# One core, a retention layer with an fp4 feed-forward: the attention output kept with its columns on partitions

## What is computed

```python
q, k = rope(x @ Wq), rope(x @ Wk)                  # 8 heads of 16
v, g = x @ Wv, x @ Wg                              # 8 heads of 32, together 256 columns
decay = where(diff >= 0, exp2(diff * s_head), 0)   # causal, one rate per head
o = (q k^T * 16**-0.5 * decay) v                   # no softmax
o = o * rsqrt(mean(o * o, over the head's 32) + 1e-5) * g_norm_w
attention = (o * silu(g)) @ Wo
ffn = fp4(silu(fp4(x1) Wgate^T) * (fp4(x1) Wup^T)) Wdown^T   # weights fp4 too, blocks of 16, width 352
```

## Time and profile before

| | us |
|---|---|
| median of 3 runs | 139.93 (139.84 to 140.35) |
| the profiled execution | 139.86 |
| its span, first to last instruction | 137.9 |
| TensorE busy | 122.2 (89%) |
| VectorE busy | 112.5 (82%) |
| ScalarE busy | 98.2 (71%) |
| GpSimd busy | 96.6 (70%) |

### The profile page before, as it was taken

The page is one execution under the profiler, slowest core; times in us unless marked ns, Lnnn a source line. Parts: engine busy times, 40 slices in busy tenths (PEclk is TensorE's granted clock), DMA queues, the critical chain, the costliest instruction groups (busy, mean ns, idle before and its releaser), DMA issues.

```text
span 137.9 us, 3502 instructions
## 1 busy us (share of the span) xinstructions
PE 122.2 (89%) x1224; PEld 78.1 (57%) x1224; DVE 112.5 (82%) x391; ACT 98.2 (71%) x311; POOL 96.6 (70%) x139
## 2 busy tenths in 40 slices
PE   4964998999999999999999999999999958888660
PEld 4822454657556465666667675757575735445550
DVE  1269468959778899999999999999999899999710
ACT  3055266678778796887888879797888978876763
POOL 4213727877876958888787979797979797656561
PEclk9999559999999999999999999999999999999997
DMA  3899980000000000000000000000000000000022
GB/s 116 255 250 233 412 257 8 0 5 5 0 5 0 0 5 2 0 5 2 0 0 5 0 2 24 0 19 7 19 0 19 5 19 19 19 21 19 19 59 60
DMA packets 6897, 6.53 MB, mean 47 GB/s; under 512 B 864, under 2 KB 6112, under 8 KB 6752
## 3 DMA queue, kind: packets, MB, share of 16 engines
q1 hardware_dynamic: 5856, 5.56, 13.6%
q10 hardware_dynamic: 1024, 0.76, 1.7%
HBM read 5.26 MB, written 1.05 MB: 46 GB/s over the span
## 4 chain that ended last, share of the span: by engine, by line
PE 78%; DVE 9%; ACT 7%; issue 2%; POOL 2%; POOLq 1%; ACTq 0%; DVEq 0%
PE ps L338 13%; PE ps L355 8%; PE ps L483 6%; PE ps L467 6%; PE ps L395 6%; PE ps L329 5%; PE ps L460 5%; PE ps L385 4%; PE ps L474 3%; PE ps L368 3%; PE ps L411 3%; PE ps L403 2%; PE ps L420 2%; PE ps L419 2%; ACT hT L513 2%
## 5 line engine op out<-in xcount | busy, mean ns | idle before, releaser
L900 POOL TENSOR_TENSOR rstd_h<-ms,minus_half 128x8 f32<-128x8 f32 x16 | 26.4, 1649 | 8.4 <-DVE ms L765 7.7
L891 POOL TENSOR_TENSOR qk<-rope_c,rope_s 128x256 f32<-128x256 f32 x16 | 11.6, 728 | 14.4 <-DVE rope_s L742 14.3
L338 PE MATMUL ps<-w_vg,xT_sb 128*128 128x512 f32 x32 | 19.0, 676 | 0.0
L483 PE MATMUL ps<-wd_T,hT 128*128 128x128 f32 x96 | 13.6, 278 | 2.7 <-ACT hT L513 2.7
L738 DVE TENSOR_TENSOR rope_c<-ps,tabs_sb 128x256 f32<-128x256 f32 x16 | 6.8, 424 | 11.1 <-PE ps L329 11.1
L925 POOL TENSOR_TENSOR hq<-h_grid,hs 128x352 f32<-128x352 f32 x16 | 13.0, 814 | 3.0 <-DVE h_grid L678 3.0
L514 ACT ACTIVATE q_eo<-ps,consts 128x128 f32<-128x128 f32 x32 | 11.8, 370 | 3.5 <-PE ps L347 3.5
L355 PE MATMUL ps<-q_eo,kT 32*128 32x256 f32 x128 | 12.0, 444 | 2.5 <-ACT q_eo L514 2.5
L483 PEld LDWEIGHTS ps<-wd_T,hT 128*128 128x128 f32 x96 | 12.1, 193 | 3.5 <-DVE r L792 2.6
L513 ACT ACTIVATE raw<-ps 128x512 f32<-128x512 f32 x16 | 9.6, 599 | 6.1 <-PE ps L355 6.1
L895 POOL TENSOR_SCALAR_AFFINE_SELECT probs<-raw 128x512 f32<-128x512 f32 x16 | 10.2, 637 | 5.0 <-ACT raw L513 5.0
(11 more groups left out here) (112 smaller groups left out, 363.5 us busy)
## 6 DMA issues: line engine op xcount, KB each, us to landing
tabs_sb<-rope_tables SPq DMA_DIRECT2D x1, 1024.0 KB, 11.4
out<-x SPq DMA_DIRECT2D x16, 64.0 KB, 1.5
tabs_sb<-rope_tables SPq DMA_DIRECT2D x1, 640.0 KB, 8.0
xT_sb<-x_transposed SPq DMA_DIRECT2D x1, 512.0 KB, 9.4
x_res<-x SPq DMA_DIRECT2D x1, 512.0 KB, 12.0
xT_sb<-x_transposed SPq DMA_DIRECT2D x1, 320.0 KB, 6.6
x_res<-x SPq DMA_DIRECT2D x1, 320.0 KB, 8.6
w_vg<-in_w_vg ACTq DMA_DIRECT2D x1, 256.0 KB, 3.4
```

The costliest lines, as they stand in the source:

```text
L338: mm(vg_ps, xT(c), w_vg[:], start=True, stop=True).then_inc(vg_pe, 1)
L483: last = mm(down_ps, hT[:, c % 2, t, :], wd_T[:, t, :], start=t == 0, stop=t == 2)
L891: gp.tensor_tensor(qk[:, c % D, :], rope_c[:, c % D, :], rope_s[:, c % D, :], ALU.add).then_inc(qk_p, 1)
L900: gp.tensor_tensor(rstd_h[:, c, :], ms[:, c, :], minus_half[:], ALU.pow).then_inc(rms_p, 1)
```

## The change

The attention output stays with its columns on partitions. The transposes of o and y and the copies around them go. ScalarE squares oT straight from PSUM; TensorE sums each head's squares with a product against a 0/1 matrix of four columns (`mean_squares`; the sums have the rows of the chunk on partitions); VectorE adds the epsilon, GpSimd takes the power as before, ScalarE spreads each head's factor over its 32 columns (`spread_rstd`), TensorE transposes that (`transpose_rstd`), and VectorE multiplies it with the gated output (`gated_output`), which is yT directly. g is therefore computed transposed too, by two products with g's weights as the stationary side. MB is 1: VectorE masks two heads, ScalarE and GpSimd handle six. Four warm-up products follow the transposes of qk for chunks 0, 1 and 2. The lists of steps of all four engines are in a new order, with new offsets, and LAST is 31.

```diff
...
 HB = I // BLK
-MB = 2
+MB = 1
 EPS = 1e-5
...
     g = np.exp(C * lg[head])
-    cst = np.stack([head % 2 == 0, head % 2 == 1, 1 / g, g], 1)
+    cst = np.stack([head % 2 == 0, head % 2 == 1, 1 / g, g, *(row // DV == n for n in range(4))], 1)
     return tab.astype(f), cst.astype(f)
...
         oT_ps = ps[:, 0:2, 0:C]
-        o_ps = ps[:, 2, 0:VD]
-        yT_ps = ps[:, 3, 0:VD]
+        ms_ps = ps[:, 2, 0:NH]
+        rstd_ps = ps[:, 3, 0:2 * C].rearrange("p (g q) -> p g q", q=C)
         qk_ps = ps[:, 4, 0:256]
         qkT_ps = ps[:, 4, 256:512]
-        vg_ps = ps[:, 5, :]
+        v_ps = ps[:, 5, 0:VD]
+        gT_ps = ps[:, 5, VD:].rearrange("p (g q) -> p g q", q=C)
         att_ps = ps[:, 5, 0:H]
...
-        FIRST, LAST = -2, 28
+        FIRST, LAST = -2, 31
...
                 elif tile.get(bank) == "oT":
-                    pe.wait_ge(oT_act, filled["oT"])
-                elif tile.get(bank) == "o":
-                    pe.wait_ge(gate_v, filled["o"])
-                elif tile.get(bank) == "yT":
-                    pe.wait_ge(yT_act, filled["yT"])
+                    pe.wait_ge(sq_act, filled["oT"])
+                    pe.wait_ge(gate_v, filled["oT"])
+                elif tile.get(bank) == "ms":
+                    pe.wait_ge(ms_v, filled["ms"])
+                elif tile.get(bank) == "rstd":
+                    pe.wait_ge(yT_v, filled["rstd"])
...
                 for _ in range(n):
-                    mm(ps[:, 7, 0:C], ident[:], ident[:], start=True, stop=True)
+                    mm(ps[:, 6, 0:C], ident[:], ident[:], start=True, stop=True)
...
                 free_vg_bank()
-                mm(vg_ps, xT(c), w_vg[:], start=True, stop=True).then_inc(vg_pe, 1)
+                mm(v_ps, xT(c), w_vg[:, 0:VD], start=True, stop=True)
+                for g in range(2):
+                    last = mm(gT_ps[:, g, :], w_vg[:, VD + g * H:VD + (g + 1) * H], xT(c), start=True, stop=True)
+                last.then_inc(vg_pe, 1)
                 fill(5, "vg")
...
                 fill(4, "qkT")
+                if c < 3:
+                    warm_up(4)
...
-            def transpose_o(c):
+            def mean_squares(c):
...
                     free_scores_bank(2)
-                pe.wait_ge(oT_act, c + 1)
-                transpose(o_ps[:, 0:C], oT[:, c % 2, 0, :], ident[:])
-                transpose(o_ps[:, C:2 * C], oT[:, c % 2, 1, :], ident[:]).then_inc(tr_pe, 1)
-                fill(2, "o")
-            def transpose_y(c):
+                pe.wait_ge(d_cst, 16)
+                pe.wait_ge(sq_act, c + 1)
+                for g in range(2):
+                    last = mm(ms_ps[:, 4 * g:4 * g + 4], o_sq[:, c % 2, g, :], head_of_row, start=True, stop=True)
+                last.then_inc(ms_pe, 1)
+                fill(2, "ms")
+            def transpose_rstd(c):
...
                     free_scores_bank(3)
-                pe.wait_ge(y_p, c + 1)
-                transpose(yT_ps[:, 0:C], y[:, c % 2, 0:128], ident[:])
-                transpose(yT_ps[:, C:2 * C], y[:, c % 2, 128:256], ident[:]).then_inc(yT_pe, 1)
-                fill(3, "yT")
+                pe.wait_ge(spread_act, c + 1)
+                for g in range(2):
+                    last = transpose(rstd_ps[:, g, :], rstd_all[:, c % 2, 4 * g:4 * g + 4, :].rearrange("p h d -> p (h d)"),
+                                     ident[:])
+                last.then_inc(rstd_pe, 1)
+                fill(3, "rstd")
...
                 free_vg_bank()
-                pe.wait_ge(yT_act, c + 1)
+                pe.wait_ge(yT_v, c + 1)
                 mm(att_ps, yT[:, c % 2, 0, :], wo_s[:, 0, :], start=True, stop=False)
...
                 run = stage_runner(s)
+                run(up, -5)
+                run(transpose_h, -8)
+                run(transpose_rstd, -1)
+                run(from_state, 0)
                 run(state_product, 0)
                 run(values, 0)
-                run(transpose_y, -1)
                 run(transpose_xq, -4)
-                run(down, -8)
-                run(transpose_o, 0)
                 run(transpose_qk, 1)
                 run(out_projection, -1)
+                run(mean_squares, 0)
+                run(down, -8)
                 run(gate, -4)
...
                     transpose_down_weights()
-                run(up, -4)
                 if s == 2:
...
                 run(scores, 1)
+                run(project_qk, 2)
                 run(project_vg, 1)
-                run(transpose_h, -7)
-                run(project_qk, 2)
-                run(from_state, 1)
...
                 act.wait_ge(vg_pe, c + 1)
-                copy(v_sb[:, c % D, :], vg_ps[:, 0:VD])
-                nc.scalar.activation(silu_g[:, c % D, :], vg_ps[:, VD:2 * VD], ACT.Silu).then_inc(vg_act, 1)
+                copy(v_sb[:, c % D, :], v_ps)
+                nc.scalar.activation(silu_g[:, c % D, :, :], gT_ps, ACT.Silu).then_inc(vg_act, 1)
...
                 run = stage_runner(s)
-                if s == 1:
+                run(k_transposed, -2)
+                run(q_odd, -2)
+                run(q_even, -2)
+                run(magic_x, -6)
+                run(ln1_norm, -5)
+                if s == 5:
+                    copy_gate_up_weights()
+                run(ln2_norm, -14)
+                run(ln2_squares, -12)
+                run(silu_of_gate, -7)
+                run(copy_scores, -2)
+                run(spread_rstd, -3)
+                run(copy_v_and_silu, -2)
+                if s == 4:
                     weights_magic(1)
-                run(copy_oT, 0)
-                run(copy_yT, -1)
-                run(copy_xqT, -4)
-                run(squares, 0)
-                run(q_even, 1)
-                run(k_transposed, 1)
-                run(q_odd, 1)
-                run(magic_x, -3)
-                run(ln2_norm, -11)
-                if s == 2:
-                    copy_gate_up_weights()
+                run(copy_hT, -10)
                 if s == 3:
+                    weights_magic(0)
+                if s == 6:
                     copy_down_weights()
-                run(ln1_centre, -2)
-                run(silu_of_gate, -4)
-                run(ln2_squares, -9)
-                run(copy_scores, 1)
-                run(copy_v_and_silu, 1)
-                run(ln1_norm, -2)
-                run(copy_hT, -7)
-                if s == 0:
-                    weights_magic(0)
-                run(magic_h, -5)
+                run(magic_h, -8)
+                run(ln1_centre, -4)
+                run(squares, -2)
+                run(copy_xqT, -6)
...
-            def mean_square(c):
-                dve.wait_ge(sq_act, c + 1)
-                vec.tensor_reduce(ms[:, c, :], o_sq[:, c % 2, :, :], AX.X, ALU.add).then_inc(ms_v, 1)
+            def mean_square_eps(c):
+                dve.wait_ge(ms_pe, c + 1)
+                vec.tensor_scalar(ms[:, c, :], ms_ps, EPS, None, ALU.add).then_inc(ms_v, 1)
...
                 dve.wait_ge(sq_act, c + 1)
-                vec.tensor_tensor(gate_o[:, c % 2, :], o_ps, silu_g[:, c % D, :], ALU.mult).then_inc(gate_v, 1)
+                vec.tensor_tensor(gate_o[:, c % 2, :, :], oT_ps, silu_g[:, c % D, :, :], ALU.mult).then_inc(gate_v, 1)
+            def gated_output(c):
+                dve.wait_ge(gate_v, c + 1)
+                dve.wait_ge(rstd_pe, c + 1)
+                vec.tensor_tensor(yT[:, c % 2, :, :], gate_o[:, c % 2, :, :], rstd_ps, ALU.mult).then_inc(yT_v, 1)
...
                 run = stage_runner(s)
-                run(mean_square, -1)
-                run(gated, -1)
-                if s == 0:
+                if s == 1:
+                    weights_amax(0)
+                run(ln1_stats, -3)
+                if s == 1:
                     weights_inv(0)
-                run(x_plus_, -4)
-                run(ln1_sum, -2)
                 if s == 3:
+                    weights_grid(0)
+                run(ln2_sum, -10)
+                if s == 4:
+                    weights_plus(1)
+                run(x_plus_, -5)
+                if s == 2:
+                    weights_inv(1)
+                if s == 4:
                     weights_grid(1)
                 if s == 2:
-                    weights_plus(1)
+                    weights_ratio(1)
+                run(h_grid_, -8)
+                run(x_grid_, -5)
+                run(h_ratio_, -7)
+                run(mask_scores, -1)
+                run(ln1_aggr, -3)
+                run(x_amax, -4)
+                run(rotate, 0)
+                if s == 1:
+                    weights_amax(1)
+                run(h_product, -6)
+                run(x_inv, -4)
                 if s == 2:
-                    weights_grid(0)
+                    scale_wo()
                 if s == 1:
                     weights_ratio(0)
-                if s == 1:
-                    scale_wo()
-                run(h_grid_, -7)
-                run(x_grid_, -4)
-                run(h_ratio_, -6)
```

(97 more changed lines are left out.)

6 lines of the change are left out of this document (2 added, 4 removed).

## The result

The changed kernel takes 139.09 us in the median of 20 runs (139.04 to 139.65). The kernel before, run beside it 20 times, has 139.04 us (137.27 to 140.35). The ratio, by the executions that each kernel shows near its fastest, is 1.0065 (95% interval 1.0036 to 1.0094): slower by about 0.65%. The prediction said 138.1 us, 1.3% faster than 139.93. The time lies in the range of 136.0 to 141.2, the direction is wrong.

A forecast was written before the change was run, and what follows sets the result against it. TensorE bounds the steady part at 6.74 us per period, VectorE the end. 8.11 + 5.4 + 5.9 + 17.1 + 17.9 + 48.8 + 33.0 gives a span of 136.2, plus 1.96 makes 138.1 us; range 136.0 to 141.2.

The forecast's parts named there:

- the clock term: From scores(1) to scores(2): warm-ups keep TensorE's clock at full speed, so 5.9 us instead of 8.15, -2.2.
- 1.0 of early waits: In the stretches before the full steady periods: shorter waits on TensorE save 1.0 us in all.
- TensorE's sum: TensorE's work per full period, parts added and removed: net +0.23 us, from 6.74 to 6.97.
- The other engines: Steady part: VectorE -0.18 us per period, ScalarE -0.17, GpSimd -0.38, all hidden behind TensorE and worth nothing.
- Early periods: Chunk-to-chunk times from scores(0) to scores(8): -0.2 us in the first, -0.5 in 2 to 4, -0.3 in 5 to 7.
- The wait of 0.34 for the copy of oT: In periods 5 to 7 the o transposes waited 0.34 us for this copy; the new order removes it.
- rival 4: A new steady-part wait, state product behind h product or v's copy behind spreading: 0.3 us in seven periods, 140.2; chance 0.14.
- Periods 2 to 4: From scores(2) to scores(5): 17.1 us instead of 17.63, -0.5, as a wait goes and the first up product slides later.
- Period 0: From scores(0) to scores(1): 5.4 us instead of 5.61, -0.2, as oT's copy and transposes leave the chain.
- The end: After scores(15), where VectorE is the bound: 33.0 us, unchanged, with 1 us of doubt for the new order.
- Rival 1: The clock falls behind 13.4 us despite the warm-ups, costing some 2.9 us, 141.0 in all; chance 0.20.
- Rivals 2 and 3: The squares' sums cost 0.76 us per period, 141.8 in all, chance 0.06; or only 0.21, 135.7, chance 0.10.

The follow-up runs named there:

- e1: The kernel before plus only the four warm-up products behind the transposes of qk for chunks 0 to 2; 137.83 us.
- e6: The kernel before plus warm-up products for chunks 0 and 1 only; 137.39 us, ratio 0.9912.
- e9: The changed kernel with warm-up products for chunks 0 and 1 only; 138.56 us.
- e2: The changed kernel without the warm-up products; median 140.88 us, executions from 137.71 to 142.96.
- e7: The changed kernel with each of the two products for the squares' sums issued twice, eight passes instead of four; 146.21 us.
- e4: The changed kernel with MB = 2, so VectorE masks four heads again; 139.44 us.

## Why the prediction was wrong

**The step that failed** is first the clock term, "5.9 instead of 8.15, -2.2". Its mechanism was right: with TensorE partly idle ahead of 13.4 us the clock falls in most executions, the warm-ups fill that time and hold the clock in either kernel (e1, e6, e9), and the order and the shorter chain do not (e2). Period 1 came out at 6.06. Its size was wrong, because the whole loss of one execution was booked as a loss of the kernel. With the clock up the kernel before has a period 1 of 5.55 (e6), so the profiled execution lost 2.6 us. Of the 58 executions 13 lose about that much, 28 about 1.7, 13 nothing, and 4 stand at 142 us for a reason that is open. The prediction noted that 139.86 was 0.07 from the median of three runs and went on as if it were typical. These three all lay above 139.8, and the median of twenty was 139.04. Against executions of the kernel before that keep their clock, the term is worth 0, or less: e2 without a fall, 137.71 us, beats the changed kernel by 1.4 us, so the three groups of warm-ups cost that much where they aren't needed.

That is half of the miss. The forecast was 1.8 us below 139.93, and the two medians differ by 0.05 the other way. The median of the kernel before accounts for 0.9 of it; the other 1.0 is the changed kernel itself, 139.09 for 138.1. Against 139.04 the forecast would still have said faster. The second step that failed is "1.0 of early waits": 0.4 came, as told below.

**TensorE's sum** held. Predicted +0.23 per full period, measured 6.987 - 6.743 = +0.24. Two parts that were put at 0 cancel: 0.09 less for v and g, 0.09 more for the factors' transposes. The sums cost 0.45, and e7 gives 0.112 per pass, the open load that was taken from the v,g product. The Trainium skill, TensorE: Matmul & The Clock Gate, section LDWEIGHTS, puts a load at its stationary columns divided by 1.2 in ns, which is 107 ns for 128. The 0.112 of e7 agrees within 5 ns. That the load is what a pass costs rests on this match; no run changed the number of stationary columns.

**The other engines** were mis-sized, and it did not matter. VectorE's busy time fell from 6.42 to 6.32 (predicted 6.2), and ScalarE's rose a little instead of falling. All stay below 6.99, and e4 shows for VectorE that nothing hangs on it.

**Early periods.** Predicted for periods 5 to 7 -0.3, measured 0. The wait of 0.34 for the copy of oT went, as argued. What took its place is the state product behind the h product, 0.09 of the 0.11 per period by which the sum was short. The prediction had named that wait as rival 4 for the full periods; it came in the others, where hT does not stand between the up and the state product. Periods 2 to 4 gave 0.2 instead of 0.5; in e9, without the third group of warm-ups, they take 17.23, near the 17.1 predicted. So 0.25 of that is the third group, whose cost the prediction put into period 1 alone. Period 0 gave 0.26. With period 1's 0.16 the periods up to 7 are 0.8 above the sum, most of the distance from 103.2 to 104.14.

**The end** is 33.16 for 33.0. What lies around the span is 1.7 us and not 1.96, which gives 0.2 back.

**The rivals.** Rival 1, the clock falls all the same, did not come in any of 20 runs. Rivals 2 and 3, dear and cheap sums, are excluded by e7 and the timeline. So the absolute time came out 1.0 us above the forecast, within its own range of 137.0 to 139.3. The direction failed for two reasons of like size: the forecast was set against one execution that was not typical of its kernel, and more than half of the early gain did not come.

## What to carry to other kernels

Before a low clock in one profile is booked as a gain, look at the scatter of the runs: where they form clusters at different mean clocks, the fall comes only now and then, and the change must be set against each cluster. Fill TensorE's idle time there with spare products where it waits anyway; a group that stands on its path costs its full length. A reduction on TensorE with the data as the stationary side costs its weight loads: in fp32 about 0.11 us for each of the two passes per product, in bf16 a small part of that.

## What was not expected of the hardware

- The same program, on the same inputs, keeps TensorE's clock in some executions and loses half of it in others. In the one fall that was traced it stayed low for 6.8 us near the start and cost 2.6 us. It fell with no idle gap of over 1.1 us on TensorE, which was busy for 51% of the time from 10.0 to 13.4 us; in the traced execution of e2 it was busy for 64% of that time and the clock stayed up, as it did with the warm-ups (74 to 75%).
- Two bf16 passes with full 128-column loads follow each other and the next product within 0.05 us, 0.025 each. Between the same two starts the fp32 passes take 0.09 each, and 0.112 each when four more are added: about four times as much for a type twice as wide.
- Executions at about 142 us of the kernel before, and at 142.9 of e2, have mean clocks of 0.99 to 1.00. No profile was taken of one, and their cause is open. So is that of the rare outliers (162.9 us at a clock of 0.747 in e9; 174 us at 0.666 and 231 us at 1.00 in the kernel before).
